# Score products of a grouped-query attention as row tiles of 32 rows, with each head's operands at their own 32 partitions

## The reference

```python
q = q.reshape(Bx, Sx, N_GROUPS, R, HEAD_DIM).transpose(0, 2, 3, 1, 4)    # R = 4, HEAD_DIM = 8
k = k.reshape(Bx, Sx, N_GROUPS, HEAD_DIM).transpose(0, 2, 1, 3)          # N_GROUPS = 8
v = v.reshape(Bx, Sx, N_GROUPS, HEAD_DIM).transpose(0, 2, 1, 3)
sim = jnp.einsum('bgrsd,bgtd->bgrst', q, k) / math.sqrt(HEAD_DIM)
attn = jax.nn.softmax(sim, axis=-1)
out = jnp.einsum('bgrst,bgtd->bgrsd', attn, v)
```

## Time and profile before

| | us |
|---|---|
| median of 3 executions | 1141.22 |
| lowest and highest | 1140.1, 1143.67 |
| the profiled execution's span, first to last instruction | 1136.1 |
| PE busy in it | 1018.1 |
| DVE busy | 762.7 |
| ACT busy | 604.8 |
| `scores` on PE (512 matmuls) | 207.8 |
| `scores_t` on PE (512 matmuls) | 160.8 |
| the maximum of a product on DVE (512) | 337.3 |

### The profile page before, as it was taken

How to read it: one execution, slowest core, us unless ns; L and a number is a source line. 1 busy time by engine, 2 the same in 40 slices (tenths; PEclk the granted TensorE clock), 3 DMA queues, 4 the chain that set the end, 5 groups by cost and what they waited for, 6 DMA issues and landing times.

```text
span 1136.1 us, 17535 instructions
## 1 busy us (share of the span) xinstructions
PE 1018.1 (90%) x5780; PEld 743.6 (65%) x5780; DVE 762.7 (67%) x1591; ACT 604.8 (53%) x911; POOL 317.4 (28%) x331
## 2 busy tenths in 40 slices
PE   4998898779999846799999999999999997999995
PEld 3877776669999724555555555555555565888884
DVE  6576454556655346798899888888888846444437
ACT  6325445355565543466665666666666665444431
POOL 2005777066655500000000122222221000455441
PEclk9999999989999967899999999999999998999999
DMA  6863333354444272011111222222222124333253
GB/s 231 315 263 126 124 110 120 113 195 150 136 124 135 89 305 35 14 28 29 29 29 29 43 55 57 56 56 57 56 56 43 63 73 155 108 108 101 92 196 137
DMA packets 49140, 120.49 MB, mean 106 GB/s; under 512 B 7752, under 2 KB 24904, under 8 KB 48520
## 3 DMA queue, kind: packets, MB, share of 16 engines
q1 hardware_dynamic: 36096, 82.80, 25.5%
q0 software_dynamic: 11808, 32.37, 7.5%
q10 hardware_dynamic: 1152, 4.19, 0.9%
HBM read 72.30 MB, written 52.42 MB: 110 GB/s over the span
## 4 chain that ended last, share of the span: by engine, by line
PE 65%; DVE 16%; POOL 7%; issue 4%; ACT 3%; DMA 3%; SPq 0%; ACTq 0%; DVEq 0%; POOLq 0%
PE psum L817 11%; PE psum L838 9%; PE psum L826 7%; DVE work_f L1699 6%; POOL xg L466 5%; PE psum L633 5%; PE psum L634 4%; PE psum L635 4%; PE psum L547 3%; PE psum L548 3%; PE psum L549 3%; PE psum L619 3%; PE psum L644 2%; DVE x L1310 1%; PE psum L665 1%
## 5 line engine op out<-in xcount | busy, mean ns | idle before, releaser
L1699 DVE TENSOR_REDUCE work_f<-psum 128x1 f32<-128x512 f32 x512 | 337.3, 685 | 49.1 <-PE psum L817 46.7
L1203 ACT ACTIVATE work_f<-psum 128x1024 f32<-128x1024 f32 x172 | 169.5, 1023 | 104.9 <-PE psum L826 100.5
L817 PE MATMUL psum<-work_r 128*128 128x512 f32 x512 | 207.8, 445 | 18.9 <-DVE work_f L1699 7.0
L473 POOL DMA_INDIRECT yk<-yb,dest x134 | 131.3, 980 | 240.1 <-ACT yb L1057 206.7
L817 PEld LDWEIGHTS psum<-work_r 128*128 128x128 f32 x512 | 93.4, 190 | 133.8 <-DVE work_f L1699 71.2
L826 PE MATMUL psum<-qm,work_r 128*128 128x512 f32 x512 | 160.8, 396 | 0.9 <-ACT work_f L1203 0.8
L466 POOL DMA_INDIRECT xg<-xn,slot x112 | 108.2, 966 | 180.9 <-PE psum L853 143.5
L826 PEld LDWEIGHTS psum<-qm,work_r 128*128 128x128 f32 x512 | 93.8, 188 | 24.1 <-ACT work_f L1203 6.2
L633 PE MATMUL psum<-wexp,xbh 128*128 x268 | 102.1, 381 | 7.4 <-issue 7.2
L1203 ACT ACTIVATE pt<-psum 128x1024 f32<-128x1024 f32 x84 | 82.8, 1022 | 45.9 <-PE psum L826 42.7
L634 PE MATMUL psum<-wexp,xbh 128*128 x268 | 96.4, 360 | 0.0
(11 more groups left out here) (218 smaller groups left out, 2065.2 us busy)
## 6 DMA issues: line engine op xcount, KB each, us to landing
xb<-xg SPq DMA_DIRECT2D x67, 258.0 KB
xg<-in_pad SPq DMA_DIRECT2D x1, 10320.0 KB
yg<-yk SPq DMA_DIRECT2D x20, 512.0 KB, 9.0
stage<-in_moe SPq DMA_DIRECT2D x16, 608.0 KB
xg<-in_pad SPq DMA_DIRECT2D x1, 7224.0 KB
work_r<-work_r SPq DMA_DIRECT2D x128, 48.0 KB
work_r<-work_r SPq DMA_DIRECT2D x32, 192.0 KB
stage<-in_moe SPq DMA_DIRECT2D x16, 384.0 KB, 3.7
```

Source lines behind the costliest of these rows:

```text
L473: nc.gpsimd.indirect_dma_start(yk[l], bass.IndirectOffsetOnAxis(ap=dest[:, j % 8, i:i + 1], axis=0), yb[l][:, j % 2, i, :], None).then_inc ...
L817: nc.tensor.matmul(next_bank(pe, ("scores", n), b_mx, n + 1), qs[g % 2][:, t * P:(t + 1) * P], km[g % 4][:, r, :], start=True, stop=True). ...
L1203: nc.scalar.activation(pt[((b * NG + g) * QT + t) % 3][:, 2 * h:2 * h + 2, :], psum[:, 3 + 2 * h:5 + 2 * h, :], ACT.Exp, scale=float(HD) * ...
L1699: v.reduce_max(mx[:, s % 2, i:i + 1], ring["scores", n], AX.X).then_inc(b_mx, 1)
```

## The change

Each head's 24 rows move to a multiple of 32 partitions, and every score product of both kinds reads only its head's 32 rows, as a tile of 32 rows x 128 columns of PE at row 32r. The four planes of `km` become one, since nothing has to be masked. The maxima of head r lie on the rows 32r+24 and 32r+25. The queries of a group are stacked by four DMAs of 24 rows instead of one of 96. Transposes, projections and `values` are as they were.

```diff
-        km = [tr(R, S) for _ in range(4)]
+        km = [tr(S) for _ in range(4)]
...
                 for r in range(R):
-                    sp.dma_start(km[u % 4][24 * r:24 * r + 24, r, :].bitcast(f32),
+                    sp.dma_start(km[u % 4][32 * r:32 * r + 24, :].bitcast(f32),
                                  kc[g * HD:(g + 1) * HD].bitcast(f32)).then_inc(b_kd, 16)
...
                 if u:
-                    sp.wait_ge(b_qd, u * 16)
+                    sp.wait_ge(b_qd, u * R * 16)
...
-                sp.dma_start(qs[u % 2][0:24 * R, :].bitcast(f32),
-                             qc[g % 4 * 32:g % 4 * 32 + 32, g // 4].bitcast(f32)).then_inc(b_qd, 16)
+                for r in range(R):
+                    sp.dma_start(qs[u % 2][32 * r:32 * r + 24, :].bitcast(f32),
+                                 qc[g % 4 * 32 + r * HD:g % 4 * 32 + (r + 1) * HD, g // 4].bitcast(f32)).then_inc(b_qd, 16)
...
                 t, r = i // R, i % R
-                nc.tensor.matmul(next_bank(pe, ("scores", n), b_mx, n + 1), qs[g % 2][:, t * P:(t + 1) * P],
-                                 km[g % 4][:, r, :], start=True, stop=True).then_inc(b_sn, 1)
+                q = slice(32 * r, 32 * r + 32)
+                nc.tensor.matmul(next_bank(pe, ("scores", n), b_mx, n + 1), qs[g % 2][q, t * P:(t + 1) * P],
+                                 km[g % 4][q, :], start=True, stop=True, tile_position=(32 * r, 0)).then_inc(b_sn, 1)
...
                 for r in (2 * h, 2 * h + 1):
-                    ins = nc.tensor.matmul(psum[:, 3 + 2 * h + r % 2, :], km[g % 4][:, r, t * P:(t + 1) * P],
-                                           qm[g % 2], start=True, stop=True)
+                    q = slice(32 * r, 32 * r + 32)
+                    ins = nc.tensor.matmul(psum[:, 3 + 2 * h + r % 2, :], km[g % 4][q, t * P:(t + 1) * P],
+                                           qm[g % 2][q, :], start=True, stop=True, tile_position=(32 * r, 0))
...
-                copy(km[n], max_rows.unsqueeze(2).broadcast_to([P, R, S])).then_inc(b_km, 1)
+                copy(km[n], max_rows.broadcast_to([P, S])).then_inc(b_km, 1)
...
-                    z = mz[:, :, 24 * R:26 * R].rearrange("p t (r n) -> p t r n", n=2)
+                    z = mz.rearrange("p t (r c) -> p t r c", c=32)[:, :, :, 24:26]
```

More of the change, by code:

```diff
@@ L133, in program @@
         low = [const[:, P + 1:P + 1 + E0 * E0], const[:, P + 1 + E0 * E0:CF0 - R]]
-        max_rows = const[:, CF0 - R:CF0]
+        max_rows = const[:, CF0 - R:CF0 - R + 1]
         before, ones = const[:, CF0:CF0 + P], const[:, CF0 + P:CF0 + 2 * P]
@@ L877, in stage @@
                             pe.wait_ge(b_kd, b * (NG * R * 16) + (s + 1) * R * 16)
-                            pe.wait_ge(b_qd, b * (NG * 16) + (s + 1) * 16)
+                            pe.wait_ge(b_qd, b * (NG * R * 16) + (s + 1) * R * 16)
                     if front:
@@ L1170, in compact @@
                     if n < 2:
-                        act.wait_ge(b_qd, b1 * (NG * 16) - (1 - n) * (NG // 2) * 16)
+                        act.wait_ge(b_qd, b1 * (NG * R * 16) - (1 - n) * (NG // 2) * R * 16)
                     else:
@@ L1835 @@
     for r in range(R):
-        const[26 * R - 2 * (R - r):26 * R - 2 * (R - r) + 2, CF0 - R + r] = 1.0
+        const[32 * r + 24:32 * r + 26, CF0 - R] = 1.0
     const[:, CF0:CF0 + P] = np.triu(np.ones((P, P), np.float32), 1)
```

## The result

The changed kernel takes 1217.07 us (median of 4) against 1140.66 for the kernel before: **slower, ratio 1.068, 95% interval 1.066 to 1.071**. The forecast was 1134 in a range of 1126 to 1152. The profiled execution has a span of 1215.7 us.

A forecast was written before the change was run, and what follows sets the result against it. The prediction took PE to look full, with most products already held by the three-bank ring of DVE reductions. Its terms, -4.4 - 4.7 + 2.1 = -7.0 us, took 1141.2 to 1134 us, range 1126 to 1152.

The forecast's parts named there:

- rival 4: Throughout: with PE less busy the granted clock falls to its lower level, time above 1190 us; chance 0.02.
- Products closer together: At a stage's end, the second released product, `values` and the next product 0 come earlier: 0.22 us, 20 stages, -4.4 us.
- the far end of the bound: Row-tile spacing: neighbours run beside each other with only weight loads serial, so starts stand 0.11 us apart.
- Inside the stage: Products 3 and 9 start 0.06 and 0.12 us earlier; 0.15 us taken for 31 stages, -4.7 us.
- the ring's time: Three banks: a product may start only after the reduction three turns back, which limits how early products go.
- its 0.06 us: Product 3: it starts at 854.67 where the banks allow 854.61, so faster products shift it by 0.06 us.
- The switches, hidden in this kernel: Two new mode round trips a stage, around `maxima_t` and `outputs_t`: costed at nothing, uncovered up to 0.7 us a stage.
- The cover: At the maxima: 0.13 us of slack before product 3 is due, called thin, with product 2 about 0.4 us earlier.
- The query DMAs: At the first pair's start, four query DMA issues instead of one delay product 0: +2.1 us, bounds 0 and 2.2.
- Filling `km`: On ACT: filling takes 1.8 instead of 7.29 us, but ACT then waits for DVE, so it gains nothing.
- Rival 3: From product start to reduction: 32-row tiles deliver sooner than 0.53 us, 0.25 us a stage, giving 1126 us; chance 0.12.
- The 5.1 us outside the span: Difference of the 1141.22 us median and the profiled 1136.1 us span, in which nothing was to change.

The follow-up runs named there:

- e5: Changed kernel with every score product of both kinds reading the same rows 0 to 31, so no row tiles run beside each other: 1382.34 us.
- e12: Full-tile kernel e1 with ten of a stage's 16 DVE reductions done twice from the second stage on: 1265.9 us, ratio 1.110.
- e8: Full-tile kernel e1 with only products 14 and 15 of `scores` in each stage as 32-row tiles: 1137.4 us, ratio 0.9975.
- e11: Full-tile kernel e1 with 14 of a stage's 32 score products as 32-row tiles, steps 4 to 9 and the stage's end: 1153.75 us, ratio 1.011.
- e2: Changed kernel with `scores_t` back to full tiles on four key planes, only `scores` as 32-row tiles: 1211.9 us, ratio 1.062.
- e3: Changed kernel with `scores` back to full tiles on four key planes, only `scores_t` as 32-row tiles: 1164.46 us, ratio 1.021.
- e1: Changed kernel with keys in four planes again and both kinds of score products as full 128-row tiles, new layout and DMAs kept: 1142.43 us, ratio 1.0011.

## Why the prediction was wrong

**The step that failed is rival 4, the clock**, to which the prediction gave 0.02. It was rejected by the length of PE's gaps: a stage would have no gap over a microsecond, and it has none (the longest in the rows above is 0.75 us). But gaps are not what the clock went by. e5 has no gaps and a clock of 0.57, e12 has 15% of gaps and a clock of 0.99. The sum held the clock at 1.00, a cost of nothing; it was 0.75 in the attention, whose stretch became 75.7 us longer. The prediction took as the rule what part of 440 to 480 us shows: a low clock where PE waits, for 1.5 to 3.1 us at a time (the prediction says 2 to 3). No row there had PE busy with a small part of the array for long. It should have seen that the change lowers what the array does even if PE is never idle, and given this an unknown's share. That the price given, above 1190 us, holds the measured 1217 is partly luck: the rival reckoned with a less busy PE, which e5 and e12 rule out as the cause. At 1.2 GHz an ordinary stage is 6.5 us longer than at 2.4.

The Trainium skill ("TensorE: Matmul & The Clock Gate", Part 1, on what is actually happening) says that the gate is set by how busy PE has been. These runs agree only if busy is not the busy time of the records: e5 and e12 contradict that reading.

The other steps, at full clock:
- **Products closer together**: right, the size by two errors that cancel. The idle time of 0.81 at a stage's start became 0.56, where 0.6 was forecast, and e8 isolates 0.24 us a stage against 0.22. But the released pair starts together, not 0.11 us apart as its loads had: the second product comes 0.34 us earlier, beyond the far end of the bound. About 0.10 of it goes again between that product and `values`: from the pair's release to `values` pass 0.43 us (649.47 to 649.90) instead of 0.67 (850.07 to 850.74).
- **Inside the stage**: right in kind, too small. Forecast 0.15 us. The one ordinary stage at full clock gives 13.24 - 12.67 = 0.57 in all, so 0.33 inside; e11 puts 0.20 of it on the steps 4 to 9. The term missed product 1: reduction 1 had waited for it within a merged row, and the three reductions at a stage's start went from 2.08 to 1.89 us. So reduction 1 ended later than the 0.64 us of the sum have it, product 3 already sat on the ring's time, and its 0.06 us were a misreading.
- **The switches, hidden in this kernel**: right at full clock, the transposes wait for DVE (0.63 us) and product 3 is not late. The cover was not thin: product 2 starts 0.35 us after product 0 instead of 1.49 (639.09 to 639.44, 852.59 to 854.08), 1.1 us earlier and not 0.4. Their price without cover, 0.6 to 0.7 us a stage for two, was measured as 0.67 in e5; e2 and e3 show what eight more do.
- **The query DMAs**: too large. From the first key DMA's issue to product 0 it was 6.80 us before (431.83 to 438.63) and is 8.17 now (433.19 to 441.36), so 1.4 and not 2.1 us: the smaller DMAs land 2.3 us after their last issue instead of 3.1.

```profile
433.19 2.91 SPq L378 DMA_DIRECT2D work_r<-work_r  x4
436.21 2.82 SPq L392 DMA_DIRECT2D work_r<-work_r  x4
439.13 2.82 SPq L378 DMA_DIRECT2D work_r<-work_r  x4
...
441.36 0.79 PE L819 MATMUL psum<-work_r 32*128 32x512 f32 x2 [4.50 <-DMA work_r<-work_r]
```

- **Filling `km`**: nothing, as forecast; e1 fills all four planes again and is not slower beyond its DMAs.
- **Rival 3, a product done sooner**: no. From a product's start to its reduction pass 0.54 and 0.53 us (639.09 to 639.63, 642.44 to 642.97), as before.
- **The 5.1 us outside the span**: they cancel in the sum, but they are not all outside the span. An execution here lasts 1.8 us longer than its span (1217.55 against 1215.7); the rest lies between two executions.

So the mechanism that was forecast is there. An estimate from these rows: 22 ordinary stages of 0.57 us less 1.4 us for the DMAs are 11 us, so at full clock throughout the kernel would take about 1130 us, near the forecast of 1134. The clock then costs some 87 us.

## What to carry to other kernels

Before masked full tiles are replaced by small row tiles, ask what else holds the clock up: zeros in a full tile are no waste if they keep the array at 2.4 GHz while another engine sets the pace. Look at the granted clock of a stage first, before its busy times, and compare stages at the same level. Row tiles are worth having at the one or two places where products wait together and something is queued behind them, as in e8; the steps between the calls of `values` gave 0.20 us a stage more (e11), and the clock took more than that back. Where row tiles and full tiles take turns the clock may hold, as in e2 and e3, but then each turn is paid for.

## What the runs showed of the hardware

- The granted clock went by the rows of the score products, not by how busy PE was: from 500 to 900 us a mean of 1.00 with 128 rows, 0.97 with 64 (one fall), 0.77 with 32, and 0.65 in e5 (490 to 1090 us), where they are 32 rows and serial. The zeros of the masked keys, over three quarters of every full tile's key rows, did not lower it (e1, 1.00); so rows that are addressed count, zeros too. Shown for this mix of products, with `values` and the transposes between them.
- It is not a fixed state of a stage. e5's stages of one shape ran at 0.50 for long and at 1.00 for others; what decides when it falls stays open. With half of the score products full it held (e2, e3), with 18 of 32 full and twelve row tiles in a row it fell at times (e11).
- Row tiles on different rows start together: two records of the first product and the second at 639.09 and 639.10, 0.01 us apart. The Trainium skill has about 4 ns for this ("TensorE: Matmul & The Clock Gate", Part 3), and the trace agrees as far as its hundredths of a us go. The same holds for a pair that is released by a wait: two records of 497 ns at 649.47 us, busy for 0.5 us together, where two full tiles started 0.34 us apart (850.07).
- From full tiles to row tiles and back costs 0.3 us or so where nothing covers it: 0.32 at the maxima of e5, 0.67 a stage for its two more trips. With one kind of product alone as row tiles a stage is 2.2 (e2) and 0.8 us (e3) longer.
